# Placing the decay exponentials of a Mamba scan elsewhere in ScalarE's order, half a block at a time

## The reference

```
q, k, v = x@Wq+bq, ctx@Wk+bk, ctx@Wv+bv          # 16 heads of 32, 257 keys
x1 = x + softmax(q k^T / sqrt(32) + mask * -1e9) v @ Wo + bo
x_, z = split(layernorm(x1) @ in_proj_w)         # 1024 channels each
x_ = silu(causal_conv4(x_) + conv_b)
bcd = x_ @ x_proj_w                              # B, C: 16 states; dt row
dt = softplus(bcd[..., -1:] * dt_w + dt_b)
dA = exp(dt[..., None] * -exp(A_log))            # the decays
dBx = (dt * x_)[..., None] * B
h = dA_t * h + dBx_t;  y_t = sum_n h_n C_n       # scan over 32 steps
x2 = x1 + ((y + x_ * D) * silu(z)) @ out_proj_w
out = x2 + quantised_ffn(layernorm(x2))
```

## Time and profile before

| | |
|---|---|
| median of 3 runs | 2639.7 us (2638.91 to 2640.65) |
| the profiled execution's own time | 2638.91 us, its span 2637.1 us |
| PE busy | 2053.5 us, 78% |
| DVE busy | 2059.9 us, 78% |
| ACT busy | 1655.0 us, 63% |
| POOL busy | 411.4 us, 16% |
| mean granted clock of TensorE | 0.891 |
| share of the chain that ended last | PE 31%, DVE 31%, ACT 22% |

### The profile page before, as it was taken

One profiled execution on the slowest core, in us unless ns is written; L12 is line 12 of the kernel. 1 busy time (PEld: TensorE's weight loads), 2 busy tenths in 40 slices (PEclk: granted clock), 3 DMA queues, 4 the chain that ended last, 5 costly groups with the idle time before them and its releaser, 6 DMA issues.

```text
span 2637.1 us, 36824 instructions
## 1 busy us (share of the span) xinstructions
PE 2053.5 (78%) x11444; PEld 1407.4 (53%) x11452; DVE 2059.9 (78%) x2507; ACT 1655.0 (63%) x4598; POOL 411.4 (16%) x296
## 2 busy tenths in 40 slices
PE   6798887878878878888787888787887878541287
PEld 4565655556556556565555655555655556321133
DVE  2433887878787979888787878797987878899686
ACT  2437565767675766767576667577676767675182
POOL 1000121111121211211211212121121122100004
PEclk9999898989998989989898999898998989765599
DMA  7502011101111010101010011111010111200013
GB/s 222 191 34 64 15 58 29 54 27 30 43 38 48 30 56 26 58 19 55 30 53 26 25 48 30 56 28 57 21 58 25 53 28 44 72 34 24 24 56 111
DMA packets 78591, 131.97 MB, mean 50 GB/s; under 512 B 16640, under 2 KB 40080, under 8 KB 73360
## 3 DMA queue, kind: packets, MB, share of 16 engines
q1 hardware_dynamic: 78480, 130.83, 15.6%
HBM read 113.63 MB, written 17.18 MB: 50 GB/s over the span
## 4 chain that ended last, share of the span: by engine, by line
PE 31%; DVE 31%; ACT 22%; issue 10%; POOL 2%; SPq 1%; DMA 1%; DVEq 1%; ACTq 0%; POOLq 0%
DVE hb L1388 9%; ACT dA L1073 8%; PE bank L743 6%; DVE hb L1399 6%; DVE hb L1393 6%; PE bank L846 5%; PE bank L874 4%; PE bank L753 4%; PE bank L829 3%; DVE hb L1384 3%; PE bank L910 2%; POOL stats L1117 2%; ACT Pr L981 2%; PE bank L792 2%; DVE xs L1344 2%
## 5 line engine op out<-in xcount | busy, mean ns | idle before, releaser
L1388 DVE TENSOR_TENSOR_SCAN hb<-dA,hb 128x2048 f32<-128x2048 f32 x128 | 568.8, 4443 | 125.4 <-ACT dA L1073 122.8
L1073 ACT ACTIVATE dA<-dt,A_sb 128x124 f32<-128x124 f32 x2048 | 604.7, 385 | 43.8 <-DVE hb L1388 29.2
L743 PE MATMUL bank<-ctxT,wk_sb 128*128 128x256 f32 x2048 | 523.5, 420 | 136.4 <-ACT ctxT L946 136.4
L743 PEld LDWEIGHTS bank<-ctxT,wk_sb 128*128 128x128 f32 x2048 | 431.2, 214 | 216.6 <-ACT ctxT L946 82.1
L753 PE MATMUL bank<-wv_sb,ctxT 128*128 128x512 f32 x1024 | 465.4, 598 | 0.7 <-ACT ctxT L946 0.7
L1399 DVE TENSOR_TENSOR hb<-hb 128x1024 f32<-128x1024 f32 (+2 forms) x384 | 300.9, 783 | 13.1
L1117 POOL TENSOR_SCALAR stats<-stats 128x1 f32<-128x1 f32 x48 | 152.2, 3171 | 984.5 <-DVE stats L1196 984.5
L1393 DVE TENSOR_TENSOR hb<-hb,BC 128x2048 f32<-128x2048 f32 x128 | 296.1, 2313 | 4.6 <-issue 0.3
L1384 DVE TENSOR_TENSOR hb<-u,BC 128x2048 f32<-128x2048 f32 x128 | 292.8, 2287 | 2.6 <-DVE u L1368 0.3
L753 PEld LDWEIGHTS bank<-wv_sb,ctxT 128*128 128x128 f32 x1024 | 186.2, 192 | 191.3 <-issue 189.0
L846 PEld LDWEIGHTS bank<-xn2T,win_sb 128*128 128x128 f32 x2048 | 238.1, 196 | 23.4 <-ACT xn2T L1009 15.8
(11 more groups left out here) (136 smaller groups left out, 2554.9 us busy)
## 6 DMA issues: line engine op xcount, KB each, us to landing
ctx_sb<-in_ctx_dram SPq DMA_DIRECT2D x64, 512.0 KB, 3.5
BC<-bcd_dram SPq DMA_DIRECT2D x32, 1024.0 KB, 5.0
maskb<-in_mask_Bx1x1xS_fk_dram SPq DMA_DIRECT2D x64, 128.5 KB, 3.2
wstage<-in_L_ffn_w_dram SPq DMA_DIRECT2D x4, 2048.0 KB, 11.3
x_sb<-in_x_dram SPq DMA_DIRECT2D x16, 256.0 KB, 3.5
win_sb<-in_L_attn_in_proj_w_dram SPq DMA_DIRECT2D x1, 4096.0 KB, 27.6
x_dram<-x SPq DMA_DIRECT2D x16, 256.0 KB, 2.0
xn_dram<-xn3T SPq DMA_DIRECT2D x16, 256.0 KB, 2.6
```

Source lines behind the costliest of these rows:

```text
L743: last = pe.matmul(bank[6 + j][:, (m % 2) * KF:(m % 2 + 1) * KF], wk_sb[:, c, m * P:(m + 1) * P], ctxT[:, c, :], start=(c == 0), stop=(c = ...
L1073: last = act.activation(dA[:, c % 2, n * BT:(n + 1) * BT, 1:], dt[:, c, :].rearrange("p (b s) -> p b s", s=S)[:, :, 1:], ACT.Exp, scale=A_ ...
L1388: ins = dve.tensor_tensor_scan(flat, dA[:, c % 2].rearrange("p n s -> p (n s)"), flat, 0.0, ALU.mult, ALU.add)
```

## The change

Two tables are replaced, and a call `place("p")`, between the transposes of the probabilities and the values in each step b, goes. The same exponentials are computed, with the same waits; only where they stand in ACT's queue is new, and most blocks are now split into their halves.

```diff
-        FINISH_DECAYS = {(0, "p"): ((5, 0), (5, 1)), (1, "p"): ((6, 0), (6, 1)), (1, "d"): ((7, 0), (7, 1))}
-        BEGIN_DECAYS = {(2, "w"): ((0, 0), (0, 1)), (2, "e"): ((1, 0), (1, 1)), (3, "p"): ((2, 0), (2, 1)),
-                        (3, "w"): ((3, 0), (3, 1)), (3, "e"): ((4, 0), (4, 1))}
+        FINISH_DECAYS = {(0, "b"): ((4, 1),), (0, "c"): ((5, 0),), (0, "d"): ((5, 1),), (0, "e"): ((6, 0),),
+                         (1, "b"): ((6, 1),), (1, "c"): ((7, 0),), (1, "d"): ((7, 1),)}
+        BEGIN_DECAYS = {(2, "w"): ((0, 0), (0, 1)), (2, "d"): ((1, 0),), (2, "e"): ((1, 1),), (3, "b"): ((2, 0), (2, 1)),
+                        (3, "c"): ((3, 0),), (3, "d"): ((3, 1),), (3, "e"): ((4, 0),)}
...
                     if here:
                         part.transpose_p(g)
-                    place("p")
```

## The result

The changed kernel took 2749.1 us (median of 4 runs, 2748.38 to 2749.63) against 2639.6 us in the runs beside it: ratio 1.0416, 95% interval 1.0404 to 1.0429. It is 4.2% slower. The forecast was 2742 us in a range of 2692 to 2780. The profiled execution's span is 2747.5 us, 110.4 more than before.

A forecast was written before the change was run, and what follows sets the result against it. DVE was taken to bound step 0, a chain through ACT and PE steps 2 and 3. 14 intervals at 6.6 us (92.4), -2 and +13.2 made 103.6 on 2638.9: 2742 us, range 2692 to 2780.

The forecast's parts named there:

- c4, +10.1: Step 0: c4's second half stands behind the convolution's taps, so its scan starts 10.1 us late; bounds 9.5 and 12.7.
- the interval without attention: c4's half behind ACT's evacuation of w1 makes its scan 18.3 us late; with gains at c5 and c1, +13.2.
- c5 and c6, -4.15: Step 1: the scan of c6 waits 0.7 us instead of 4.85, gaining 4.15; DVE is then 6.0 us late.
- The lost cover: Decays no longer run while PE weighs values; ctxT of step 2 stays 10.1 us late, decays of c0 6.6.
- a further 1.0 for slow keys in step 2: PE's gap of about 2.2 us before these keys may bring the low clock; 1.0 us taken.
- c1, -2.37: Step 2: c1's first half is hidden ahead of the silu of z, taking 2.37 us off the path to the context copies.
- Step 3: The 1.86 us wait for c2 goes, but PT waits for c2; Wo is late, x1 3.4 us late.
- For the clock I had 2.2 on top: Step 3: low clock after PE's gap of about 3.3 us costs the weighing and Wo 2.2 us.
- my sum had 11.1: Step 3: weighing starts at 1150.5, not 1143.03; oT ends at 1157.6, Wo at 1161.3; 2.2 us of low clock come on top.
- The sum per interval: Loop interval: x1 3.4 us late plus 3.2 for TensorE's clock, 6.6 us.
- The first interval with scans: No back part and no late c4; it gains the 2.4 us of c1, taken as -2.
- 2805: Time under the rival "slower still": all three PE gaps at low clock, 11.1 us per interval; chance 0.13.

The follow-up runs named there:

- Experiment 2: Kernel before with one edit: second half of c4 behind the taps of step 0; 2842.6 us, ratio 1.0772.
- 9: Changed kernel with c4 whole at the end of step 3 and c2 behind PTl again; 2637.1 us, ratio 0.9990.
- experiment 4: Changed kernel with c2 behind PTl in step 3 again; 2747.3 us, ratio 1.0410.
- Experiment 6: Kernel before with one edit: first half of c1 ahead of the silu of z in step 2; 2605.7 us, ratio 0.9870.
- experiment 5: Changed kernel with 20 idle transposes on PE ahead of the weighing of step 3; 2750.4 us, ratio 1.0418.
- table of four: c4 whole or half behind the taps, by c2 behind PTl or ahead of PT: 2637 (9), 2704 (experiment 1), 2747 (experiment 4), 2749 us (the change).
- experiment 1: Changed kernel with all of c4 at the end of step 3 again; 2704.0 us, ratio 1.0245.
- experiment 7: Kernel before with a new order, decays only where ACT stands idle; 2561.2 us, ratio 0.9702.
- 10: Kernel before with step 3 alone as changed: c2 ahead of PT, c3 in halves around oT, c4 whole; 2697.9 us, ratio 1.0211.
- 3: Changed kernel with both halves of c7 together ahead of oT of step 1; 2785.0 us, ratio 1.0552.
- 8: Experiment 4 with 30 idle transposes on PE in step 0, between keys and transposes of the normed rows; 2774.0 us, ratio 1.0503.
- 11: Experiment 7 with 20 idle transposes on PE in step 0; 2515.4 us, ratio 0.9528.
- 12: 11 with 45 more idle transposes on PE in step 3, ahead of the wait for xnT; 2531.4 us, ratio 0.9587.

## Why the prediction was right

The direction, the mechanism and the size held: 103.6 us forecast, 109.5 measured. The size is in part good luck, as some terms were off and one wait was missed.

- *c4, +10.1.* Measured: 9.67 late in the loop and 17.9 us, against 18.3, in the interval without attention. In the loop I let the keys of step 0 end 0.6 us earlier after x1; they ran at full clock and ended 1.0 earlier. Experiment 2 shows that this edit alone makes the kernel slower, and 9 with 4 that it does so in the changed one.
- *c5 and c6, -4.15.* Measured: 9.67 - 5.35 = 4.3, with 0.61 us of wait left against 0.7.
- *The lost cover.* I had c0 6.6 us late through ctxT, PE and V, and a further 1.0 for slow keys in step 2. It was 7.9 late, but by another way, which I missed: L1357 waits for all decays of the tile before, and the half of c7 at (1,d) ends after DVE is ready. 2.50 us of wait there and 5.35 from before make 7.9. The keys of step 2 ran at full clock (7.17 us). ctxT, the start of the way that I had, was 9.3 us late against 10.1, but the keys behind it ended at 1129.62, and ACT came to KT only at 1132.24, without a wait for PE. So that step failed in its cause, while its sum stood.
- *c1, -2.37.* Experiment 6 has it by itself: 2.3 us per interval. In the changed kernel Q is 4.8 late after c0 at 7.9; of the 3.1 between, some 2.4 are c1's, and the rest came from the queries, which took 5.26 us and not 6.07.
- *Step 3.* The wait for c2 went, Wo became late and x1 waits 3.74 us for it, as said. With half of c3 ahead of oT and no low clock I had 7.1 us from the weighing to the end of oT, and Wo right behind it; experiment 5 has 7.1 to Wo where the clock was kept. For the clock I had 2.2 on top, and it cost 3.0, so this term was 0.8 too small, while the 1.0 for the keys of step 2 was for nothing. Of the 3.3 us that the stretch from L789 to L803 grew, PE's own slow matmuls are all: oT ended at 1195.05, PE came to Wo at 1195.83. Wo so began 11.2 us later after x1 than before; my sum had 11.1.
- *The sum per interval.* 6.6 forecast, 6.88 measured. Where I went wrong was in adding the parts. In the table of four the costs of c4 and c2 do not add (110, 67, together 112). In experiment 4, of x1's wait of 3.74 us, half went to the wait for c2 and the other half was lost to a low clock elsewhere. By my sum, putting c4 back should have given 5 to 9 us per interval; it gave 2 (experiment 1).
- *The first interval with scans.* -2 forecast, +0.8 measured (134.4 against 133.6, from x1 to x1). It is 131.9 in experiments 4 and 9, with c2 behind PTl, and 134.5 in experiment 1, with c2 ahead of PT: that cost of 2.6 I had left out. That c1 gained 2 there is not shown: experiment 6, with c1 alone, has 134.0, and experiment 2, without it, 131.9.
- *TensorE's clock.* The low clock came after the gap of 3.06 us, and not after the one of 1.92 ahead of the keys of step 2 (4.41 before), though in experiment 1 the same keys took 8.86 us after 1.93 in every second interval. By the section "HAM oscillation" of the Trainium skill's page TensorE: Matmul & The Clock Gate, bursts with waits between them bring the low clock back. The trace agrees for the first of the two gaps and not for the second.
- *The range.* Half of the way from 2742 to 2805 is 2774, and not 2780; nothing hangs on it.

What stays open: why the intervals of a loop settle on a length that repeats within 0.1 us, or on a pattern of two to four (137.1 and 139.3 in experiment 7), and why kernels with different waits share one. The single lengths lie 3.4 us apart: 143.4 (before and 9), 146.8 (10), 150.2 (the change and 4), 153.6 (3) and 157.0 us (2). So a part that is worth a microsecond or two can read as nothing or as 3.4 us in each interval, some 48 in all. The table of four, and "nothing came back" in experiment 4, are to be read with that in mind. That the place of the low-clock stretches takes part is borne out by the traces (4, 5, 8); that it is all, is not shown.

## What to carry to other kernels

Work off the bound belongs where its engine waits anyway, ahead of that wait and not ahead of what others wait for: half a block moved earlier so gained 1.3% alone, half a block moved later behind the taps cost 7.7% alone. Where several engines are bound by turns, don't add up the waits that a change makes or takes away, but try its parts apart and together. And look at a moved instruction from both sides: who waits for its result, and who waits for it to have read its input.

## What the runs showed of the hardware

In the changed kernel a gap of 3.06 us on PE cost 3.0 us in the matmuls behind it; after one of 1.9 us the keys took 7.17 us in one kernel and 8.86 in another (1). Filling one gap with idle transposes did not simply remove the low clock. 20 of them, 2.35 us of PE's time, in step 0 made one order 46 us faster (11); 20 in step 3 of the changed kernel kept the clock there in every second interval and gained nothing in all (5); 30 in step 0 kept it in five intervals of 14, and the kernel was 27 us slower than without them (8); 45 more at a second place made the fastest kernel 16 us slower (12). In these runs, where the low clock falls depended on more than the gap just ahead.

The mean granted clock doesn't tell such a change's worth: it was 0.891 before and 0.893 in the 4.2% slower kernel. Only the ends stand out, 0.850 in the slowest kernel (2) and 0.918 to 0.931 in the runs of the two fastest (11, 12).
